# Encoder attention in 64-token chunks on smaller TensorE tiles, outputs turned by VectorE

## What is computed

```python
for l in range(6):
    q, k, v = (x @ W[l] + b[l] for W, b in ((Wq, bq), (Wk, bk), (Wv, bv)))   # 16 heads of 16
    q, k = elu(q) + 1, elu(k) + 1
    # per head, causal, no softmax (chunks of 128 in the reference):
    num = tril(q @ k.T) @ v + q @ (k.T @ v of the chunks before)
    den = the same with v replaced by ones, + 1e-6
    x = layer_norm(x + (num / den) @ Wo[l] + bo[l])
    x = layer_norm(x + gelu(x @ W1[l] + b1[l]) @ W2[l] + b2[l])
```

## Time and profile before

| what | value |
|---|---|
| median of 3 runs | 1611.46 us (1610.8 to 1612.81) |
| span of the profiled execution | 1609.4 us |
| TensorE matmuls, busy | 1523.1 us, 95% |
| TensorE weight loads, busy | 1225.0 us, 76% |
| VectorE, busy | 1287.7 us, 80% |
| ScalarE, busy | 951.3 us, 59% |
| GpSimd, busy | 802.8 us, 50% |
| mean granted TensorE clock | 0.986 |
| chain that ended last | TensorE 83%, VectorE 11%, the rest 6% |

### The profile page before, as it was taken

One profiled execution on the slowest core, in us unless ns is written; L12 is line 12 of the kernel. 1 busy time (PEld: TensorE's weight loads), 2 busy tenths in 40 slices (PEclk: granted clock), 3 DMA queues, 4 the chain that ended last, 5 costly groups with the idle time before them and its releaser, 6 DMA issues.

```text
span 1609.4 us, 38530 instructions
## 1 busy us (share of the span) xinstructions
PE 1523.1 (95%) x15894; PEld 1225.0 (76%) x15894; DVE 1287.7 (80%) x2566; ACT 951.3 (59%) x1516; POOL 802.8 (50%) x580
## 2 busy tenths in 40 slices
PE   3799999999999999999999999999998999999998
PEld 3688888888888888888888888888886566666434
DVE  3777888888888888888878878888776788988556
ACT  3465556665556665565655556655534777777445
POOL 3354445545455454554555535654455366664424
PEclk8899999999999999999999999999999999999999
DMA  6110011201121001210012100112024444443001
GB/s 137 37 62 15 21 24 41 66 9 21 25 67 46 5 19 24 67 47 11 12 24 67 47 19 11 18 41 50 1 49 121 138 136 139 143 139 95 1 0 53
DMA packets 98351, 82.52 MB, mean 51 GB/s; under 512 B 23040, under 2 KB 86400, under 8 KB 98176
## 3 DMA queue, kind: packets, MB, share of 16 engines
q1 hardware_dynamic: 98176, 80.06, 18.5%
HBM read 50.78 MB, written 14.68 MB: 41 GB/s over the span
## 4 chain that ended last, share of the span: by engine, by line
PE 83%; DVE 11%; issue 2%; ACT 1%; SPq 1%; POOL 1%; DMA 0%; ACTq 0%; DVEq 0%
PE e_pr L170 10%; PE e_pr L172 8%; PE e_pr L171 8%; PE e_tr L428 6%; PE e_sc L401 6%; PE x_psO L1366 4%; PE e_tr L170 4%; PE e_tr L172 3%; PE e_tr L171 3%; PE e_sc L170 3%; PE e_sc L172 3%; PE e_sc L171 3%; PE e_tr L438 3%; PE x_psT L1351 2%; PE f_bank L1912 2%
## 5 line engine op out<-in xcount | busy, mean ns | idle before, releaser
L715 POOL TENSOR_TENSOR e_h_lo<-e_h_f,e_h_hi 128x512 fp32r<-128x512 f32 x192 | 265.7, 1388 | 279.1 <-ACT e_h_hi L557 275.2
L805 DVE TENSOR_TENSOR e_am<-e_sc,c_amask 128x1024 f32<-128x1024 f32 x192 | 225.7, 1216 | 18.3 <-PE e_sc L401 18.3
L556 ACT ACTIVATE e_h_f<-e_pr,e_h_bias 128x512 f32<-128x512 f32 x192 | 132.1, 688 | 174.3 <-PE e_pr L172 170.6
L1676 DVE TENSOR_REDUCE x_mx<-x_psS 128x4 f32<-128x1024 f32 x128 | 150.9, 1219 | 25.8 <-PE x_psS L1329 24.9
L170 PE MATMUL e_tr<-e_W_hi,e_h_hi 128*128 128x256 f32 x576 | 163.2, 283 | 8.1 <-DVE X L762 8.1
L170 PE MATMUL e_pr<-e_yT_hi,e_W_hi 128*128 128x512 f32 x384 | 168.6, 439 | 0.0
L171 PE MATMUL e_tr<-e_W_lo,e_h_hi 128*128 128x256 f32 x576 | 160.8, 279 | 0.0
L172 PE MATMUL e_tr<-e_W_hi,e_h_lo 128*128 128x256 f32 x576 | 160.7, 279 | 0.0
L172 PE MATMUL e_pr<-e_yT_hi,e_W_lo 128*128 128x512 f32 x384 | 152.3, 397 | 0.0
L171 PE MATMUL e_pr<-e_yT_lo,e_W_hi 128*128 128x512 f32 x384 | 151.8, 395 | 0.0
L1502 ACT ACTIVATE x_ex<-x_psT 128x1024 f32<-128x1024 f32 x128 | 130.9, 1022 | 26.5 <-PE x_psT L1351 21.6
(11 more groups left out here) (284 smaller groups left out, 4320.5 us busy)
## 6 DMA issues: line engine op xcount, KB each, us to landing
e_raw_m<-in_L_attn_W_dram SPq DMA_DIRECT2D x12, 1024.0 KB, 5.3
x_qs<-query_rows SPq DMA_DIRECT2D x48, 256.0 KB
e_x_raw<-e_a_tok SPq DMA_DIRECT2D x368, 32.0 KB, 1.9
x_ks<-key_rows SPq DMA_DIRECT2D x48, 128.0 KB, 2.8
query_rows<-x_q_hi SPq DMA_DIRECT2D x16, 256.0 KB, 2.1
query_rows<-x_q_lo SPq DMA_DIRECT2D x16, 256.0 KB, 2.3
x_ctok<-in_ctx_dram SPq DMA_DIRECT2D x8, 256.0 KB, 3.3
x_xo<-in_x_dram SPq DMA_DIRECT2D x8, 256.0 KB, 3.8
```

Of the source, the lines that this page charges most:

```text
L556: act.activation(h_f[:, m % HR, :], ps_pr[m % 2][:, :], ACT.Gelu, bias=h_bias[:, m:m + 1])
L715: pool.tensor_tensor(h_lo[:, m, :], h_f[:, m % HR, :], h_hi[:, m, :].bitcast(F32), ALU.subtract).then_inc(h_lo_done, 1)
L805: dve.tensor_tensor(am[:, s % 2, c, :, :, :], ps_sc[:, :, c * 2 * P:(c + 1) * 2 * P].rearrange("p r (h n) -> p r h n", n=P), amask[:, :].u ...
L1676: dve.tensor_reduce(mx[:, N % 2, :, 0:HG].rearrange("p i (a h) -> p h a i", a=2)[:, pair], ps_s[pair][:, :, :].rearrange("p a (i j) -> p a ...
```

## The change

- Scores and masks use chunks of 64 tokens. Four masked products of 64 x 64 a slice and row tile take the place of 128 x 128: half the elements. Three states a pair of slices (`STATES` = 3: for the second chunk of the first slice, and for both chunks of the second) carry the rest; `kv` and the key-value products grow from 16 to 64 matmuls, key transposes from four to eight.
- Scores are plain float32, unsplit: `k_hi`, `k_lo`, `qx_hi`, `qx_lo` go; `qx` (the queries, once for each head of a pair) stays. The stationary side has 64 columns, so the tiles are 32x64.
- `scores(b)` and `attend(b)` work on two slices at once (`NPAIR` = 2). State products use 32x32 tiles on the diagonal, value products 64x32 tiles, 64 columns streamed.
- `out_copy`, `to_tokens` and the transposes back are gone. VectorE turns the output from PSUM in blocks of 32 (`turn`), divides, and turns it back (`divide`); ScalarE makes `aT_hi` (`output_hi`), VectorE `aT_lo` (`output_lo`).
- The order: TensorE runs `attend(0)`, `scores(1)`, `mlp_up(2)` to `mlp_up(4)`, `attend(1)`, `mlp_up(5)` to `mlp_up(7)`, the projection of the first pair, `qk(0)`, the projection of the second pair. ScalarE runs both `x_hi` of the next tile right behind the key copies, ahead of `yT_hi`. VectorE runs `x_lo` of the next tile right behind `yT_lo`.

The core of the diff. TensorE:

```diff
-                    for b in range(2):
-                        for c in range(KC):
-                            mm = pe.transpose(ps_pr[0][:, blk(b * KC + c)], qkT[:, KC + c, blk(2 * b + 1)], ident[:, :])
-                    mm.then_inc(ktr_full, 1)
+                    for late in range(2):
+                        bank = ps_sc[:, LATE_BANK, :] if late else ps_pr[0][:, :]
+                        for b in range(NPAIR):
+                            for c in range(KC):
+                                mm = pe.transpose(bank[:, blk(b * KC + c)], qkT[:, KC + c, blk(2 * b + 1 - late)], ident[:, :])
...
                         for c in range(KC):
-                            for r in range(NR):
-                                rows = slice(r * RH, (r + 1) * RH)
-                                mm = pe.matmul(ps_sc[rows, KV_BANK[b], c * 2 * HX:(c + 1) * 2 * HX], ktok[:, b, c, rows],
-                                               vx[:, 2 * b + 1, c * HC + 2 * r:c * HC + 2 * r + 2, 0:HX], start=True, stop=True,
-                                               skip_group_check=True)
-                        mm.then_inc(kv_full, 1)
+                            for state in (1, 2):
+                                for r in range(NR):
+                                    rows = slice(r * RH, (r + 1) * RH)
+                                    pe.matmul(state_bank(rows, b, state, c), ktok[:, 0, b, c, rows], values_of(slice(0, P), 2 * b + 1, c, r),
+                                              start=(b == 0 and c == 0 and state == 1), stop=(state == 1), skip_group_check=True)
+                    late_rows = slice(CH, P)
+                    for b in range(NPAIR):
+                        for c in range(KC):
+                            for state, late in ((0, 0), (2, 1)):
+                                for r in range(NR):
+                                    rows = slice(r * RH, (r + 1) * RH)
+                                    mm = pe.matmul(state_bank(rows, b, state, c), ktok[late_rows, late, b, c, rows],
+                                                   values_of(late_rows, 2 * b + 1 - late, c, r), start=False, stop=True, skip_group_check=True)
+                    mm.then_inc(kv_full, 1)
                 if mlp:
...
+                    for s in (2 * b, 2 * b + 1):
+                        for c in range(KC):
+                            for late in range(2):
+                                for r in range(NR):
+                                    rows = slice(r * RH, (r + 1) * RH)
+                                    at = ((s % 2) * KC + c) * P
+                                    mm = pe.matmul(ps_sc[late * CH:(late + 1) * CH, r, at:at + P], qkT[rows, KC + c, chunk(s, late)],
+                                                   qx[rows, c, :, chunk(s, late)], start=True, stop=True, skip_group_check=True)
                     mm.then_inc(sc_full, 1)
...
+                    for s, late, state in ((2 * b, 1, 1), (2 * b, 0, 2), (2 * b + 1, 0, 0)):
                         for c in range(KC):
+                            for p in range(2):
+                                for r in range(NR):
+                                    rows = slice(r * RH, (r + 1) * RH)
+                                    pe.matmul(out_block(s, late, c, p)[rows, :], kv[rows, (b * STATES + state) * KC + c, p, :],
+                                              qkT[rows, c, chunk(s, late)], start=(s == 2 * b and c == 0 and p == 0), stop=False,
+                                              skip_group_check=True)
+                    for s in (2 * b, 2 * b + 1):
+                        pe.wait_ge(am_done, SB * t + s + 1)
+                        for c in range(KC):
+                            for p in range(2):
+                                for late in range(2):
+                                    tokens = slice(late * CH, (late + 1) * CH)
+                                    for r in range(NR):
+                                        mm = pe.matmul(out_block(s, late, c, p)[HP * r:HP * (r + 1), :], vx[tokens, s, c * HC + 2 * r + p, :],
+                                                       am[tokens, s % 2, r, c * 2 + p, :], start=False, stop=True, skip_group_check=True)
                     mm.then_inc(out_full, 1)
 
...
@@ -445,42 +479,31 @@
                     mlp_up(1)
                 if u == final:
                     cross.x1_transpose(0, cross.early(1))
-                for s in range(SB):
-
-                    if attn and s + 1 < SB:
-                        scores(s + 1)
-                    if attn:
-                        attend(s)
-                    if mlp:
-                        mlp_up(2 + s)
-                    if u == final and s == 0:
-                        cross.queries(0, 0, cross.early(2))
-                    if attn:
-                        to_tokens(s)
+                if attn:
+                    attend(0)
+                    scores(1)
                 if mlp:
+                    mlp_up(2)
+                if u == final:
+                    cross.queries(0, 0, cross.early(2))
+                if mlp:
+                    mlp_up(3)
+                    mlp_up(4)
+                if attn:
+                    attend(1)
+                if mlp:
+                    mlp_up(5)
                     mlp_up(6)
+                    mlp_up(7)
                 if attn:
-
-                    pe.wait_ge(a_done, SB * t + SB)
-                    for c in range(KC):
-                        for s in range(SB):
-                            mm = pe.transpose(ps_tr[c][:, blk(s)], a_tok[:, s, blk(c)], ident[:, :])
-                        mm.then_inc(aT_tr, 1)
-                if mlp:
-                    mlp_up(7)
+                    project_out(0)
                 if following and mlp:
                     pe.wait_ge(qkv_lo, (t + 1) // NT + 1)
                     pe.wait_ge(xT_lo_done, 2 * t + 4)
                     pe.wait_ge(gelu_done, FC * u + FC - 1)
                     qk(0)
                 if attn:
-                    pe.wait_ge(o_lo, la + 1)
-                    pe.wait_ge(aT_lo_done, 2 * t + 2)
-                    for s in range(SB):
-                        for c in range(KC):
-                            mm = split3(pe, ps_sc[:, s, 0:D], (aT_hi[:, c, blk(s)], aT_lo[:, c, blk(s)]),
-                                        (hi["Wo"][:, c, :], lo["Wo"][:, c, :]), c == 0, c == KC - 1)
-                        mm.then_inc(wo_full, 1)
+                    project_out(1)
 
             steps(step)
             cross.queries(0, 1, cross.early(3))
...
```

ScalarE:

```diff
+
+                def key_tokens(late):
+                    act.wait_ge(ktr_full, 2 * t + late + 1)
+                    rows = slice(late * CH, P)
+                    bank = ps_sc[rows, LATE_BANK, :] if late else ps_pr[0][rows, :]
+                    act.activation(ktok[rows, late, :, :, :].rearrange("p b c n -> p (b c n)"), bank, ACT.Copy).then_inc(ktok_done, 1)
+
+                def output_hi(b):
+                    act.wait_ge(aT_done, NPAIR * t + b + 1)
+                    act.activation(aT_hi[:, b, :, :], aT[:, b, :, :], ACT.Copy).then_inc(aT_hi_done, 1)
 
                 if attn:
                     if q < 0:
-                        act.wait_ge(attn_set, 6)
+                        act.wait_ge(attn_set, 7)
                     for c in range(KC):
-                        head_pair_hi(c)
+                        head_pair(c)
+                    for late in range(2):
+                        key_tokens(late)
+                if following:
+                    act.wait_ge(v_full, 2 * t + 2)
                     for c in range(KC):
-                        key_hi(c)
-                    act.wait_ge(ktr_full, t + 1)
-                    act.activation(ktok[:, :, :, :], ps_pr[0][:, :].rearrange("p (b c n) -> p b c n", b=2, c=KC),
-                                   ACT.Copy).then_inc(ktok_done, 1)
+                        x_hi(t + 1, c)
                 if u == final:
                     cross.weights()
                     cross.context(0, cross.early(3))
...
```

VectorE (`turn`, `divide` and their order):

```diff
+                def turn(b):
+                    dve.wait_ge(out_full, NPAIR * t + b + 1)
+                    dve.transpose(turned[:, :], ps_tr2[:, :, :].rearrange("p k n -> p (k n)")).then_inc(turned_done, 1)
+
+                def divide(b):
+                    n = NPAIR * t + b
+                    o = turned[:, :].rearrange("p (h d) -> p h d", d=HP)
+                    dve.wait_ge(turned_done, n + 1)
+                    dve.tensor_scalar(den[:, :].unsqueeze(2), o[:, :, DH:HX], DEN_EPS, None, ALU.add).then_inc(den_step, 1)
+                    dve.wait_ge(den_step, 4 * n + 1)
+                    dve.reciprocal(rden[:, :], den[:, :]).then_inc(den_step, 1)
+                    dve.wait_ge(den_step, 4 * n + 2)
+                    for p in range(2):
+                        dve.tensor_tensor(quotient[:, :].rearrange("p (g j h d) -> p g j h d", j=2, h=2, d=DH)[:, :, :, p],
```

(27 more changed lines are left out.)

255 lines of the change are left out of this document (101 added, 154 removed).

## The result

The change makes the kernel slower: 1824.37 us (1822.19 to 1828.1, 4 runs) against 1611.95 us (1610.8 to 1612.81), a ratio of 1.1324 with a 95% interval of [1.1303, 1.1345]. The profiled execution has a span of 1822.6 us, 213.2 more than before, and a mean granted clock of 0.945 for 0.986. The prediction had the direction and not the size: 1636, and a range that ended at 1692.

What follows compares the result with a forecast made beforehand. TensorE's queue bounds a step. Ordinary steps -3, layer-first +12, step 22 -2.8, prologue and step 0 -2, clock +10 and +10: together +24 on 1609.4, 1633, plus 2 gives 1636 us; range 1592 to 1692.

Steps and rivals of the forecast that it cites:

- the hold's mechanism: x_hi, moved ahead of yT_hi, waits for the next tile's DMAs; TensorE idles some 2.6 us ahead of mlp_up(0).
- M: Start of a step's first feed-forward matmul, mlp_up(0); forecast at T + 25.2 in ordinary steps, T + 21.3 before.
- The landing: Arrival of the next tile's transposed x by DMA, forecast at T + 21.9; x_hi waits for it.
- T: Start of a step's second-query-block matmul on TensorE, from which the forecast counts times; an ordinary step was forecast at 48.2 us.
- rival 2: Faster: the wait for x is mostly hidden, steps cost 45.6 us, about 1545 (half hidden 1590); chance 0.15.
- From M to the next T: TensorE's second part of a step, forecast at 23.0 us, 4.1 less than before the change.
- the division as hidden: VectorE's second-pair chain was to end near M + 20.6, just ahead of the last projection at M + 21.5.
- Its own sign of being wrong: Forecast wrong if mlp_up(0) starts without a wait, or M to next T is 25 us or more, or under 22.
- Eight tiles side by side: Small score and value matmuls on TensorE run eight at once: 1.14 us a pair for scores, 1.05 for values.
- Rival 3: Small matmuls on TensorE pack only four tiles at once: 2.2 us more a step, 1676; chance 0.12.
- Rival 4: Instructions reach TensorE too slowly, 16 to 21 ns per weight load and matmul in attend: 1690 to 1720; chance 0.13.
- The clock: TensorE's clock falls after stalls: half the ordinary steps at 1.3 us, +10, and six long stalls at 1.7, +10.

Runs made afterwards that it cites:

- o: j with den and its reciprocal rden in PSUM instead of SBUF, all work done: 1602.29 us.
- a: The changed kernel with both x_hi back behind gelu(3) on ScalarE and x_lo ahead of turn(1) on VectorE: 1720.05 us.
- c: a with attend cut in two and feed-forward blocks between the runs of small matmuls on TensorE: 1695.16 us.
- i: c with VectorE's centre(2) moved ahead of turn(0) and half of scale(2) ahead of mask(2): 1648.76 us.
- j: i with the first pair's output projection moved behind qk(0) on TensorE: 1640.76 us.
- d: The changed kernel with work left out: GpSimd computes 8 of 512 columns of each h_lo from the second step on: 1747.35 us, one run.
- b: The kernel before with only both x_hi of the next tile moved ahead of the yT_hi casts on ScalarE: 1755.3 us.

## Why the prediction was wrong

The 213 us, and 9 more, can be laid out along one chain of complete kernels, from after (1824.4) to o (1602.3): hold -104 (a), runs spread -25 (c), layer norm out of the division's way -46 (i), projection moved -8 (j), `den` and `rden` in PSUM -38 (o). In another order the shares would differ: PSUM alone is worth 54 on after, and d's edit 77 there and 61 on c.

- **The direction and the hold's mechanism: right, the direction partly by luck.** `x_hi` waits for the DMA, then `yT_hi`, `yT_lo`, `mlp_up(0)`; from 668.99, where x is there, to M are 3.24 us (forecast 3.3). The landing was late by 1.5: T + 23.4 for T + 21.9. The transpose came at T + 9.0 for T + 8.4, and 16 issues took 11.75 us for 10.90. So M = T + 26.7 for T + 25.2. A term of the sum mis-sized: 1.6 in the mean of the 16 ordinary steps and 2.6 in the five layer-first ones, some 38 us. But the direction did not hang on it: without the hold (rival 2) the prediction had 1545, and a, without it, took 1720, still 7% slower than before.
- **From M to the next T, 23.0 us: the step that failed.** The sum put the stops of the instruction supply at nothing, took the division as hidden, and had too few falls of the clock. Its own sign of being wrong was 25 or more. This one took 31.4, and the mean of the ordinary steps is 30.0; over 16 steps at 7.0 and five layer-first ones at 7.7 beyond their forecast these are some 151 of the 188 us that the forecast lacks, with the 20 that it had under the clock to be taken off. In the step shown: two stops 3.35; two stretches at the lower clock, 6.97 us that did 3.6 us of work, 3.3; the wait for `aT_lo` 1.14: together 7.8, and 0.6 are left. The two stops had a rival of their own and were left out of the sum; that the division hides was a step of the sum. It stood near M + 20.6 as against a need at M + 21.5, with 0.9 us of slack, and shows no prices for `den` and the quotient. The divide of before, the nearest row for them, reads PSUM (the quotient, L818, 424 ns in the mean there, 868 in after). In o, with neither hold nor collisions in the division, the part takes 25.4 in the mean, and the whole is worth 9 us against before, not the 66 of rival 2.
- **Eight tiles side by side: right.** 64 scores records last 1.21 (1.14 forecast), 96 state records 1.47 from start to start (1.5), 128 value records 1.42 (1.05: the one that came out dearer). Rival 3 falls: four at a time would have taken 2.0 for the scores and 1.9 for the values.
- **Rival 4, the supply of instructions: right in kind, wrong in form.** It was worked out as a price an instruction, 16 to 21 ns a pair. A run of value or state products goes at 11 to 15 ns a pair until what was fetched is used up, and then stands for some 1.5 us. L350's 32 pairs were too short a run to show that.
- **The clock: too low.** The sum took half the ordinary steps at 1.3, 20 us in all. After has 157 us more at the lower level than before, which at half the speed is some 79 us (an estimate, idle time in these stretches included). b, with nothing but the hold, lost about 50 us beyond its waits. The row at 2.15 us without a fall was read as a hint for stalls of 2.6; they were 4.4 in the mean (96.5 / 22). The stop of 1.65 us was followed by no fall (the next wide matmuls keep 0.50 and 0.40 us), the one of 1.70 was: in this case the length of a stop alone doesn't tell.
- **VectorE beside GpSimd: missing.** No rival had it. The divide of before reads PSUM, so its rows could not show it; the layer norm's instruction (L795, 787 ns in after, 540 in d) has the same wait. Before's trace had it too, in `x_lo`, whose row (2.38 for two) the prediction used as it stood. Its shortest, median and longest in ns, and those of `yT_lo`, which has the same size but reads PSUM:

```profile
L837 DVE TENSOR_TENSOR e_xT_lo<-e_x_raw,e_xT_hi x46: 681/1191/1780, 58.6 to 1131.2; 128x512 fp32r<-128x512 f32 x46
...
L798 DVE TENSOR_TENSOR e_yT_lo<-e_tr,e_yT_hi x48: 678/686/693, 79.7 to 1201.0; 128x512 fp32r<-128x512 f32 x48
```

The 28 that began while GpSimd was at work took 1579 in the mean, the other 18 took 682. A look at how much the lengths of one instruction differ within before would have led there.

## What to carry to other kernels

Before a cast or a copy that waits for a DMA is moved up an in-order queue, count what stands behind it. Price a run of many small matmuls by its instructions as well as by its columns, and put large ones between; and give an engine's short dependent steps an operand in PSUM, or a time when GpSimd is quiet, if they stand on the path. When a chain is forecast to hide by under a microsecond, count its cost in the sum and don't rely on its being hidden.
